# Scratch of queries and keys doubled by parity, and another order of the calls on every engine and on the DMA queue

## The reference

```python
h = _layernorm(x, axis=-1) * (1 + ca) + sa
x = x + ga * _L0_attn_ref(h, wq, bq, wk, bk, wv, bv, wo, bo)
h = _layernorm(x, axis=-1) * (1 + cb) + sb
x = x + gb * _L0_ffn_ref(h, gate_w, w1, w2, w3, w1s, w2s, w3s)

# attention: allowed where |i - j| <= 32
scores = jnp.einsum('bhqd,bhkd->bhqk', q, k) * scale + bias
out = jnp.einsum('bhqk,bhkd->bhqd', softmax(scores), v) @ wo.T + bo

# experts: top 2 of 8 by softmax of x @ gate_w.T
h = silu(xe @ w1[e]) * (xe @ w3[e]);  out = out + h @ w2[e]
```

## Time and profile before

| | us |
|---|---|
| median of 3 runs | 745.36 |
| lowest and highest | 744.31, 747.26 |
| the profiled execution | 746.85 |
| its span, from first to last instruction | 745.1 |

### The profile page before, as it was taken

The page is one execution under the profiler, slowest core; times in us unless marked ns, Lnnn a source line. Parts: engine busy times, 40 slices in busy tenths (PEclk is TensorE's granted clock), DMA queues, the critical chain, the costliest instruction groups (busy, mean ns, idle before and its releaser), DMA issues.

```text
span 745.1 us, 18977 instructions
## 1 busy us (share of the span) xinstructions
PE 660.5 (89%) x5934; PEld 558.9 (75%) x5934; DVE 581.2 (78%) x1541; ACT 613.0 (82%) x2602; POOL 541.2 (73%) x564
## 2 busy tenths in 40 slices
PE   2267798999989999999899999989899989979886
PEld 1155677878878887878788887878788878878765
DVE  5446667988969898989889898969798888867553
ACT  4276779998979999999999899979899998875442
POOL 4430418887868989788878888868968886758784
PEclk9996557999989999999999999999999999999999
DMA  4747586777676777777677878577777676713120
GB/s 147 181 97 189 131 203 183 187 214 192 181 184 186 200 205 199 190 213 184 175 187 213 204 195 214 163 197 200 189 187 204 161 201 174 188 41 136 64 83 14
DMA packets 193860, 127.70 MB, mean 171 GB/s; under 512 B 110640, under 2 KB 170848, under 8 KB 193632
## 3 DMA queue, kind: packets, MB, share of 16 engines
q1 hardware_dynamic: 193760, 126.50, 64.3%
HBM read 96.29 MB, written 30.17 MB: 170 GB/s over the span
## 4 chain that ended last, share of the span: by engine, by line
PE 42%; DMA 22%; SPq 13%; POOL 8%; issue 6%; ACT 5%; DVE 3%; POOLq 0%; DVEq 0%; ACTq 0%
DMA k<-k_scr 15%; PE ps_s L1209 11%; PE ps_Y L1277 10%; SPq L315 8%; DMA r_scr<-rst 6%; PE ps_O L1232 5%; ACT p L675 4%; SPq L323 3%; PE ps_A L1152 3%; POOL xl L495 3%; POOL xs L489 2%; PE ps_M L1260 2%; PE ps_A L1153 2%; PE ps_A L1154 2%; PE ps_B L1152 2%
## 5 line engine op out<-in xcount | busy, mean ns | idle before, releaser
L675 ACT ACTIVATE p<-ps_s,nmx 128x96 f32<-128x96 f32 x1024 | 332.3, 345 | 58.4 <-DVE nmx L878 57.8
L675 ACT ACTIVATION_READ_ACCUMULATOR p<-ps_s,nmx 128x1 f32 x1024 | 215.7, 211 | 0.0
L1209 PE MATMUL ps_s<-k,q 128*128 128x96 f32 x1024 | 167.2, 297 | 54.1 <-DMA k<-k_scr 42.2
L1209 PEld LDWEIGHTS ps_s<-k,q 128*128 128x128 f32 x1024 | 147.6, 210 | 81.4 <-DMA k<-k_scr 50.2
L878 DVE TENSOR_REDUCE nmx<-ps_s 128x4 f32<-128x384 f32 x256 | 138.0, 548 | 67.4 <-PE ps_s L1209 64.0
L495 POOL TENSOR_TENSOR xl<-xs,xh 128x512 fp32r<-128x512 f32 x128 | 163.4, 1282 | 20.7 <-ACT xh L697 20.7
L489 POOL TENSOR_TENSOR xs<-h,sbc 128x512 f32<-128x512 f32 x128 | 164.0, 1287 | 4.1 <-DMA sbc<-s_scr 4.1
L1277 PE MATMUL ps_Y<-w2s,g 128*128 128x128 f32 x1152 | 163.4, 290 | 0.6 <-DVE g L984 0.6
L1277 PEld LDWEIGHTS ps_Y<-w2s,g 128*128 128x128 f32 x1152 | 150.2, 202 | 4.7 <-DVE g L984 0.8
L895 DVE STREAM_TRANSPOSE pt<-p 128x384 f32<-128x384 f32 x256 | 136.1, 558 | 6.1 <-PE ps_O L1232 4.4
L975 DVE SCALAR_TENSOR_TENSOR th<-th,ps_A 128x512 f32<-128x512 f32 x144 | 97.7, 678 | 36.2 <-ACT th L718 36.1
(11 more groups left out here) (119 smaller groups left out, 920.4 us busy)
## 6 DMA issues: line engine op xcount, KB each, us to landing
sbc<-s_scr SPq DMA_DIRECT2D x64, 512.0 KB, 5.6
k<-k_scr SPq DMA_DIRECT2D x64, 384.0 KB
q<-q_scr SPq DMA_DIRECT2D x128, 96.0 KB
k<-k_scr SPq DMA_DIRECT2D x32, 336.0 KB
q_scr<-qh SPq DMA_DIRECT2D x32, 256.0 KB, 2.5
k_scr<-kh SPq DMA_DIRECT2D x32, 256.0 KB, 2.6
xt<-x SPq DMA_DIRECT2D x16, 256.0 KB, 6.0
q_scr<-ql SPq DMA_DIRECT2D x16, 256.0 KB, 2.5
```

The lines of the kernel that those rows point to most:

```text
L675: last = nc.scalar.activation(p[:, n % PRING, gg, :], ps_s[:, n % 2, MK * gg:MK * gg + MK], ACT.Exp, bias=nmx[:, n, gg:gg + 1], accum_out= ...
L1209: last = mm(ps_s[:, n % 2, MK * gg:MK * gg + MK], heads[:, h, gg, nl], k4[:, h, gg, :, MB * nl:MB * nl + MB], start=gg == 0, stop=gg == HG ...
```

## The change

The scratch becomes two copies of itself, taken by the parity of the item, and put_q waits for the halves of the item two before. On SP, store comes behind the loads of the first half and load_ga behind load_x and load_bias. On the other engines the calls of a turn are put in another order. No instruction is added or taken away apart from waits: `project_k` now waits for hl too, and `high_h1` for q_mm, since project_k comes first of the two.

```diff
-        q_scr = nc.dram_tensor("q_scr", (HJ, 3, 32, S), F32, kind="Internal").ap()
-        k_scr = nc.dram_tensor("k_scr", (HJ, 3, 32, S), F32, kind="Internal").ap()
+        q_scr = nc.dram_tensor("q_scr", (2, HJ, 3, 32, S), F32, kind="Internal").ap()
+        k_scr = nc.dram_tensor("k_scr", (2, HJ, 3, 32, S), F32, kind="Internal").ap()
...
-            def put_q(b, loaded):
+            def put_q(b, par):
...
-                if loaded is not None:
-                    sp.wait_ge(half_in[0], loaded)
-                    sp.wait_ge(half_in[1], loaded)
+                if b >= 2:
+                    sp.wait_ge(half_in[0], 112 * (b - 1))
+                    sp.wait_ge(half_in[1], 112 * (b - 1))
...
+                if has(b, -1, 1):
+                    put_q(b + 1, 1 - par)
+                    put_k(b + 1, 1 - par)
+                    load_half(b + 1, 0, 1 - par)
                 if has(b, 3):
                     store(b - 3)
-                if has(b, -1, 1):
-                    put_q(b + 1, loaded)
-                    put_k(b + 1)
-                    load_half(b + 1, 0)
-                    load_ga(b + 1)
                 if has(b, -2, 2):
                     load_x(b + 2)
                     load_bias(b + 2)
+                if has(b, -1, 1):
+                    load_ga(b + 1)
```

More of the change, by code:

```diff
@@ L559, in body @@
                     inverse(b + 1, l1, ln1)
+                if has(b, 2):
+                    scaled(b - 2, 1, par)
+                if has(b, -1, 1):
                     shift(b + 1, l1, ln1)
                 if has(b, 2):
-                    scaled(b - 2, 1, par)
                     scaled_low(b - 2, 0, par)
@@ L1044, in body @@
                 if has(b, 0):
-                    turn_p(b, 1)
                     turn_p(b, 2)
-                    turn_p(b, 3)
+                    maximum(b, 4)
                 if has(b, 3):
@@ L1051, in body @@
                 if has(b, 0):
-                    maximum(b, 4)
+                    turn_p(b, 3)
+                if has(b, 0, 1):
+                    turn_v(b)
+                if has(b, 0):
                     maximum(b, 5)
@@ L1076, in body @@
                     moments(b - 1, l2, ln2)
+                if has(b, 2):
+                    half_silu(b - 2, 2, par)
+                if has(b, 0):
+                    maximum(b, 8)
+                    maximum(b, 9)
+                if has(b, 2):
+                    combine(b - 2, 2, par)
                 if has(b, -1, 1):
@@ L1079, in body @@
                 if has(b, 0):
[L1080 to L1084, removed]
                     turn_p(b, 5)
-                    maximum(b, 9)
+                    turn_p(b, 6)
                 if has(b, -1, 1):
@@ L1112, in body @@
                     maximum(b, 12)
+                    maximum(b, 13)
                 if has(b, 1):
                     route_top(b - 1)
-                if has(b, 0):
-                    maximum(b, 13)
+                if has(b, 2):
+                    half_silu(b - 2, 4, par)
                 if has(b, 1):
@@ L1119, in body @@
                 if has(b, 2):
-                    half_silu(b - 2, 4, par)
+                    combine(b - 2, 4, par)
                 if has(b, 1):
                     route_index(b - 1)
-                if has(b, 2):
-                    combine(b - 2, 4, par)
-                if has(b, 1):
                     route_select(b - 1)
                 if has(b, 0):
+                    turn_p(b, 11)
                     maximum(b, 14)
-                    turn_p(b, 11)
                     turn_p(b, 12)
-                    turn_p(b, 13)
                     maximum(b, 15)
@@ L1307, in body @@
                     scores(b, 0)
-                if has(b, 3):
-                    down(b - 3, 4, 1 - par)
-                if has(b, 0):
                     scores(b, 1)
+                if has(b, 1):
+                    values(b - 1, 12)
                 if has(b, 3):
@@ L1319, in body @@
                     down(b - 3, 5, par)
+                    expert(b - 3, 7)
                 if has(b, 0):
                     scores(b, 3)
+                    scores(b, 4)
+                if has(b, 1):
+                    values(b - 1, 14)
                 if has(b, 3):
-                    expert(b - 3, 7)
                     down(b - 3, 6, 1 - par)
-                if has(b, 0):
-                    scores(b, 4)
-                if has(b, 3):
                     expert(b - 3, 8)
@@ L1334, in body @@
                     expert(b - 2, 0)
+                if has(b, 1):
+                    values(b - 1, 15)
+                if has(b, -1, 1):
+                    flip(b + 1, l1, ln1, "M1")
                 if has(b, 3):
                     down(b - 3, 8, 1 - par)
[L1337 to L1340, removed]
                 if has(b, 2):
                     expert(b - 2, 1)
-                if has(b, -1, 1):
-                    flip(b + 1, l1, ln1, "M1")
                 if has(b, 0):
@@ L1365, in body @@
                     values(b, 2)
+                    scores(b, 10)
                     values(b, 3)
+                    values(b, 4)
                 if has(b, 1):
@@ L1387, in body @@
                 if has(b, 0):
+                    values(b, 8)
                     scores(b, 14)
@@ L1401, in body @@
                     values(b, 11)
-                    values(b, 12)
+                if has(b, 2):
+                    down(b - 2, 4, par)
             pipeline(pe, body)
```

76 lines of the change are left out of this document (37 added, 39 removed).

## The result

The changed kernel takes 767.1 us in the median (763.3 to 771.6, 4 runs) against 746.3 for the kernel before, a ratio of 1.0256 with a 95% interval of 1.0207 to 1.0305. It is slower, by 20.8 us where 18.1 were forecast. The profiled execution took 770.76 us, its span is 769.0 us.

The account below looks back on a forecast made before the run. A ring of DVE, SP and DMA work, not PE, was taken to set the turn; 11.1 + 9.6 + 2.6 - 5.2 gave +18.1 us, 765.0 us as profiled or 763.5 against the median, range 744 to 786.

Parts of the forecast that it names:

- A ring: Closed chain from X through first key load, score spreading and rt to the next X: 40.64 us, PE no link of length.
- X: The moment PE starts scores(b, 8), the first of the second half; it repeated every 40.54 us.
- The doubling at 0: Two scratches free put_q's wait for both halves; costed at 0, because low_q needs X in the new order.
- DVE around X: low_q behind both maxima and combine delays the put of kl and the loads: 0.85 us a turn, bounds 0.6 and 1.3.
- the clock: Longer PE waits at X bring stretches at a lower clock: 0.2 us a turn, bounds 0 and 0.8.
- k0: The first key load of the next item's first half, on SP's queue, 9.16 us after X.
- store: Its 256 KB now lie ahead of the s_scr write: 0.8 us in 12 turns, bounds 0.5 and 1.5.
- copy_sums: Copy ahead of probabilities 1 on ACT lets r_scr issue earlier: 0.4 us a turn won, bounds 0 and 1.2.
- the spreading: The 2 MB of loads sbc<-s_scr on SP's queue; from there to rt took 8.13 us.
- The rival in which r_scr's landing follows its own issue: Transfers not kept in order, so r_scr lands 3.2 us after issue and store costs nothing: 726 us, chance 0.13.
- The rest at 0: Other reordered calls, mostly between T (start of scores(b, 0)) and X, costed at 0, covered by PE's 1.96 us slack.
- What would show it: Signs: kl put 5.0 to 5.5 after X, PE's wait at scores 8 over 3 us, turns of 42 us.

Follow-up runs that it names:

- b_sbc: Kernel before, spreading only 256 of each 1024 routing scores from the second item on, so experts use stale scores: 712.5 us, ratio 0.9492.
- b_double: Kernel before with the scratch doubled alone, all orders as before: 743.6 us, ratio 0.9907.
- the cut: Loads of sbc for experts 4 to 7 moved behind the next turn's second-half loads; alone on the kernel before: 721.7 us, ratio 0.9589.
- b_dve: Kernel before with nothing but the new order of DVE around X: 769.7 us, ratio 1.0332.
- a_lowq: Changed kernel with the old order of DVE around X put back: 749.1 us, ratio 0.9951 to the kernel before.
- a_split: Changed kernel, complete, with the spreading of the routing scores cut in two: 746.4 us, ratio 0.9898 to the kernel before.
- b_store: Kernel before with only store moved behind the first half's loads and load_ga: 754.8 us, ratio 1.0094.

## Why the prediction was right

**What bounds the kernel** was right. A ring sets the turn, and not PE's work: with less ahead of r_scr the turn falls from 40.50 to 37.97 us, PE's own 37.9. That PE is no link of it was not right. The issue of s_scr goes by PE and ACT, 15.2 us behind X, and the key loads count only through its landing. I had put 29.5 us, or a little more where the clock falls, as the most to be won; b_sbc won 5%, 38 us, and there the low stretches of the clock went with the waits: its granted clock from 131 to 590 us is 1.00, against 0.98 before.

**The doubling at 0** was said of the new order, with low_q behind X as its cover, and that tie is there (SP waits 38.0 us for ql). b_double has low_q ahead of X, and there the doubling wins 7 us, as the prediction said that it would without the tie; what failed is the theory put down for b_double, that kl behind DVE is cover enough. No run takes the doubling out of the changed kernel, so whether it is worth 0 there stays open. Under the cut the doubling gives nothing that can be seen (0.9607 against 0.9589), which fits a gain through the ring, but with intervals of 0.5% to each side doesn't show it.

**DVE around X** had the right mechanism and too small a price. Its term was 0.85 a turn with 0.2 for the clock, 13.7 us. The runs give 3.1 to 3.3%, 23 to 25 us. DVE's own delay was sized well: low_k is done at X + 4.75 before and at X + 5.29 after in the mean of the 12 turns, 0.54 later where the sum had 0.6. (low_q ends at X + 3.55 in the turn shown, not at 3.44; its row has 0.75 us.) The step that was too small is what follows on SP, 0.25 in the sum: the put of kl came 0.03 us behind kl before and comes 0.82 behind it after, because the put of ql and the two of kh stand close ahead of it, and X to k0 grew by 1.49, over the bound of 1.3. In b_dve it grew by 1.85, low_k by 1.07 of it.

The clock has a part in b_dve, but not the one forecast in the changed kernel. There the waits at X did not grow by 1.3 us, they shrank from 1.56 to 1.06 in the mean, and the granted clock from 131 to 640 us is 0.99 against 0.98 before, so 0.2 a turn for the clock had no ground. In b_dve the waits grew to 1.97. Of its waits on PE of 0.8 us or more in that stretch 9 of 12 were followed by 8 us at a mean clock of 0.79 or less, against 5 of 12 before and 4 of 13 after; combine is then released later, and low_k with it. Which of the two comes first is not shown. The stretches of the kernel before and of b_dve, with their granted clock in the third column from the right:

```profile
131.00:640.00 509.00, 486.75 (x4682) 417.05 (x4682) 440.70 (x1194) 471.31 (x2044) 414.55 (x425) 0.98 0.74 194
```

```profile
131.00:640.00 509.00, 478.30 (x4466) 410.33 (x4466) 425.71 (x1146) 455.67 (x1960) 403.52 (x416) 0.96 0.70 186
```

The other part lies where I had put 0: X of b = 2 is at 131.98 in the changed kernel and at 131.48 in b_dve, against 128.05 in the earlier trace rows: the fill, the first turns, cost 3.4 to 3.9 us. Not all of it is DVE's order, as a_lowq has this X at 130.35 without it.

**store** had the right place and was sized at 9.6 us; the runs give 4 to 7, the rows 0.3 to 0.4 us a turn there, under my lower bound of 0.5, and 0.2 to 0.6 back between rt and X, for which the sum had nothing. The row that I leaned on, 0.9 us for store and grow behind the key loads, measures when store lands, not by how much a transfer behind it is put off.

**copy_sums** was sized at -0.4 a turn and won nothing by the rows; no run has it alone. r_scr is issued 1.98 us behind the spreading now instead of 3.62 (means of the same 12 turns), and rt comes 8.61 behind it instead of 8.47. The rival in which r_scr's landing follows its own issue is refuted by the same numbers, and by b_sbc, where it moved by 2.42 us and its issue by 0.31.

**The rest at 0** held for the changed kernel as a whole: without the order of DVE it is at 0.9951. But the cover had a price of its own. PE's 1.45 us a turn disappear in the ring's wait, and show in a_split, where the ring is cut.

**What would show it:** the put of kl at 5.0 to 5.5 behind X came out in four turns (5.41 to 5.43) and at 6.11 in the mean; k0 to the spreading at 11 is 10.7; turns of 42 us are 41.9; s_scr's median to landing of over 3.3 us is 5.0. PE's wait at X of over 3 us was wrong: it is 1.06 in the mean, 0.57 and 1.81 in the turn shown. PE fills the time with its longer order, with waits for hl, 0.76 in the same turn, and in some turns with waits at T. All its waits together are 2.27 us a turn against 1.84.

So the sum of +18.1 against +20.8 measured is good partly by luck: the order of DVE was some 10 us too small and copy_sums took back 5 that weren't there, while the smaller store (-3 to -6) went the other way, and with it the doubling (-7), if it wins in the new order what it wins in the old one.

## What to carry to other kernels

Where every turn has one wait for a transfer, follow the waits back until they close on themselves before costing anything: an edit counts by the piece of that ring it lengthens. Ask of each transfer on the ring what was issued ahead of it; taking 1 MB that nobody needed yet out of the way of two writes of 16 KB won 4%, more than any new order of the engines tried here. A call that was slack beside such a ring can have a price that shows as soon as the ring is shorter, so the order of an engine is to be chosen again after each such cut.

## What the runs showed of the hardware

Two writes of 16 KB behind a spreading of 2 MB were back 8.5 to 8.6 us after the spreading's first issue (before and after), whether they were issued 3.6 or 2.0 us behind it, and 5.6 to 6.3 us after it when 0.5 or 1 MB stood ahead (b_sbc and the four kernels with the cut). The write of s_scr, issued at the same time behind X, landed 1.6 us later when the key loads ahead of it were issued 1.5 us later. Issuing a transfer of 256 KB on SP took 0.60 us, but 1.34 in the turn shown when several stood close together. From 125 to 640 us, stretches of 8 us at a mean granted clock of 0.79 or less came behind waits of PE of 1.3 to 3.1 us. Of the waits of 0.8 us or more none that was shorter than that was followed by one, and not every one of that length was: in b_store waits of 2.88 and 3.06 us were followed by 1.00. I had not expected that a block of `values`, 8 matmuls, put by itself among others costs PE half as much again (0.30 against about 0.20 us).
